# Splitting a norm over two stages, moving two outputs into attention's loop, and unread products in TensorE's waits

## The reference

```
x = x + mha(layernorm(x), ctx, ctx)             # 16 heads, softmax over 64 keys
y = layernorm(x)
h = y + attention(rmsnorm(y, ln1))              # 16 heads of 32, latent q and kv, rope, causal
x = x + h + moe0(rmsnorm(h, ln2))               # 1 shared expert + top 2 of 7, inner width 256
x = x + readout(layernorm(x), ctx, mask)        # softmax(x ctx^T / sqrt(512)) ctx
x = x + moe1(layernorm(x))                      # top 8 of 32 experts, inner width 192
```

## Time and profile before

| what | us |
|---|---|
| median of 3 runs (lowest, highest) | 1833.81 (1829.18, 1837.07) |
| the profiled execution | 1838.66 |
| its span | 1836.8 |
| `cross` and the start, to 93 us: PE clock | 0.73 |
| attention up to 571 us: PE clock | 0.94 |
| 571 to 620 us, end of attention: PE clock | 0.71 |
| 931 to 1088 us, `middle`: PE clock | 0.61 |
| 1139 to 1803 us, moe1: PE clock | 1.00 |

### The profile page before, as it was taken

One profiled execution on the slowest core, in us unless ns is written; L12 is line 12 of the kernel. 1 busy time (PEld: TensorE's weight loads), 2 busy tenths in 40 slices (PEclk: granted clock), 3 DMA queues, 4 the chain that ended last, 5 costly groups with the idle time before them and its releaser, 6 DMA issues. The chain is left out here.

```text
span 1836.8 us, 34150 instructions
## 1 busy us (share of the span) xinstructions
PE 1558.3 (85%) x8796; PEld 1186.7 (65%) x8797; DVE 1360.3 (74%) x2776; ACT 1038.4 (57%) x1969; POOL 786.0 (43%) x542
## 2 busy tenths in 40 slices
PE   4577899898888599999938827999999999999991
PEld 2445667666564477777726526788888787778880
DVE  6735867756675466666637876999999999889992
ACT  1124645534452266666523315888888888788870
POOL 5100010110202323555410124788888888778881
PEclk9588999998989599999976657999999999999996
DMA  9225537344350544765574314888888889888778
GB/s 336 79 53 120 111 69 179 75 116 88 70 138 1 156 163 131 172 136 102 86 219 146 121 60 90 211 187 187 185 192 172 184 186 215 212 208 181 130 124 301
DMA packets 169997, 270.55 MB, mean 147 GB/s; under 512 B 20417, under 2 KB 96193, under 8 KB 168193
## 3 DMA queue, kind: packets, MB, share of 16 engines
q0 software_dynamic: 49008, 117.24, 32.3%
q1 hardware_dynamic: 120896, 152.18, 29.4%
HBM read 153.72 MB, written 89.06 MB: 132 GB/s over the span
## 5 line engine op out<-in xcount | busy, mean ns | idle before, releaser
L1609 DVE TENSOR_TENSOR moe_w_lo<-moe_w_up,moe_w_hi 128x1536 fp32r<-128x1536 f32 (+1 forms) x216 | 408.5, 1891 | 10.0 <-ACT moe_w_hi L1488 10.0
L1429 POOL DMA_INDIRECT moe_rows<-moe_rows,moe_ids x200 | 323.4, 1617 | 67.4 <-issue 57.9
L1488 ACT ACTIVATE moe_w_hi<-moe_w_up 128x1536 fp32r (+3 forms) x216 | 343.3, 1590 | 8.5 <-SPq L1387 8.5
L1704 PE MATMUL psum<-moe_w_hi,moe_rows_hi 128*128 128x384 f32 (+1 forms) x864 | 322.8, 374 | 6.3 <-DVE moe_rows_lo L1603 6.3
L1705 PE MATMUL psum<-moe_w_lo,moe_rows_hi 128*128 128x384 f32 (+1 forms) x864 | 304.5, 352 | 0.0
L1706 PE MATMUL psum<-moe_w_hi,moe_rows_lo 128*128 128x384 f32 (+1 forms) x864 | 304.4, 352 | 0.0
L1730 PE MATMUL psum<-moe_w_down,moe_hid_t 128*128 (+1 forms) x544 | 268.6, 592 | 1.9 <-DVE moe_tail_t L1597 1.3
L1445 POOL DMA_INDIRECT moe_sum<-moe_res,moe_ids x100 | 163.7, 1637 | 100.3 <-ACT moe_res L1531 42.7
L1445 POOL DMA_INDIRECT moe_other<-moe_res,moe_ids x100 | 166.0, 1660 | 87.6 <-ACT moe_res L1531 36.9
L1603 DVE TENSOR_TENSOR moe_rows_lo<-psum,moe_rows_hi 128x512 fp32r<-128x512 f32 x216 | 148.9, 689 | 54.6 <-issue 40.0
L721 ACT ACTIVATE prob<-psum,neg_top 128x128 f32<-128x128 f32 (+3 forms) x256 | 133.3, 528 | 85.0 <-DVE neg_top L851 75.5
(11 more groups left out here) (282 smaller groups left out, 2830.3 us busy)
## 6 DMA issues: line engine op xcount, KB each, us to landing
moe_w_up<-in_L_ffn_w_gate SPq DMA_DIRECT2D x32, 384.0 KB
moe_w_up<-in_L_ffn_w_up SPq DMA_DIRECT2D x32, 384.0 KB
q_st<-q_hi SPq DMA_DIRECT2D x64, 128.0 KB, 2.9
k_st<-k_hi SPq DMA_DIRECT2D x64, 128.0 KB, 3.1
k_st<-k_lo SPq DMA_DIRECT2D x64, 128.0 KB, 3.2
q_st<-q_lo SPq DMA_DIRECT2D x64, 128.0 KB, 3.1
moe_w_down<-in_L_ffn_w_down SPq DMA_DIRECT2D x32, 256.0 KB
moe_w_down<-in_L_ffn_w_down SPq DMA_DIRECT2D x64, 128.0 KB
```

Source lines behind the costliest of these rows:

```text
L1429: pool.indirect_dma_start(rows[u][:, :], None, d["rows"], bass.IndirectOffsetOnAxis(ids[:, t:t + 1], 0)).then_inc(gathered[u], 16)
L1488: sc.activation(w_hi[u % SPLITS][:, :], w_up[:, bass.ds(at * DC, DC), :].rearrange("p a n -> p (a n)"), ACT.Copy).then_inc(T["wh"], 1)
L1609: v.tensor_tensor(w_lo[u % SPLITS][:, :], w_up[:, bass.ds(at * DC, DC), :].rearrange("p a n -> p (a n)"), w_hi[u % SPLITS][:, :].bitcast(F ...
L1704: mm(ps[:, 2 + i, 0:2 * I], hi, w_h, start=(k == 0), stop=False)
```

## The change

Three edits in one. First, `two_norms` takes over POOL's five steps and is called twice: in `cross` for the four tiles of batch 0, as soon as DVE has their variance (in its loop's first round), and in attention's block for the other twelve, behind POOL's first memset; DVE waits for it before the first tile of batch 1. Second, the `normed(1, t)` calls move from before the loop to its first two rounds, two tiles each; and for the last batch the `output` of its first two tiles moves to steps 20 and 24 and their `residual` to steps 22 and 26, with the last tile's output in bank 0 in place of bank 3. Third, `keep_busy` adds products of the identity with 512 columns of constants, written to a PSUM bank that nobody reads then, in full or with half of the columns of the identity (and half of the bank's partitions). It stands at nine places of PE's order: 2 and 2 in attention's end, 3 and 3 at the start of moe0, 2 at that of moe1, and 5, 4, 2 (last batch only) and 2 (each of the other three batches) in `middle`, there with half. No result changes. No line that loads experts is in the diff.

```diff
+def keep_busy(nc, m, c, products, bank, half=False):
+    rows = slice(P // 2, P) if half else slice(0, P)
+    for _ in range(products):
+        nc.tensor.matmul(m["psum"][rows, bank, :], c["ident"][:, rows], m["const"][:, 0:D], start=True, stop=True)
...
+def two_norms(g, own, m, var, mv, rstd, rms, tiles):
+    var, spread, rstd, rms, power = var[:, tiles], mv[:, tiles, 1], rstd[:, tiles], rms[:, tiles], m["power"][:, tiles]
+    own.run(g.tensor_tensor(rstd, var, power, ALU.pow))
+    own.run(g.tensor_tensor(rms, rstd, rstd, ALU.mult))
+    own.run(g.tensor_tensor(rms, rms, spread, ALU.mult))
+    own.run(g.tensor_tensor(rms, rms, m["eps"][:, tiles], ALU.add))
+    return g.tensor_tensor(rms, rms, power, ALU.pow)
...
             pool.wait_ge(S["var"], 1)
-            own.run(g.tensor_tensor(rstd[:, :], var[:, :], m["power"][:, :], ALU.pow))
...
+            own.run(two_norms(g, own, m, var, mv, rstd, rms, slice(0, TPB)))
...
                 stats_of(x(t), t, mv[:, t, :])
+                if b == 0:
+                    own.wait()
+                    v.tensor_scalar(var[:, 0:TPB], mv[:, 0:TPB, 1], EPS, None, ALU.add).then_inc(S["var"], 1)
             own.wait()
-            v.tensor_scalar(var[:, :], mv[:, :, 1], EPS, None, ALU.add).then_inc(S["var"], 1)
+            own.run(v.tensor_scalar(var[:, TPB:TILES], mv[:, TPB:TILES, 1], EPS, None, ALU.add))
...
+        OUT_BANK = lambda b, n: 0 if (b, n) == (LAST, LAST) else 3
...
-            g.memset(r["prob"][:, :, :], -1.0).then_inc(S["zeroed"], 1)
+            g.memset(r["prob"][:, :, :], -1.0).then_inc(S["scales"], 1)
             pool.sem_inc(S["sent"], 1)
+            own = Steps(pool, S["scales"], 1)
+            two_norms(g, own, m, var, mv, rstd, rms, slice(TPB, TILES)).then_inc(S["scales"], 1)
...
                 dve.wait_ge(S["z"], n)
+                if n == TPB:
+                    dve.wait_ge(S["scales"], 6)
...
-                v.tensor_tensor(h[:, t, :], h[:, t, :], ps[:, 3, :], ALU.add).then_inc(S["hres"], 1)
+                v.tensor_tensor(h[:, t, :], h[:, t, :], ps[:, OUT_BANK(b, n), :], ALU.add).then_inc(S["hres"], 1)
...
+                if b == LAST and s in (22, 26):
+                    residual(LAST, s // 4 - 5)
...
-            for t in range(TPB):
-                normed(1, t)
             maxima(*UNITS[0])
             for at in range(len(UNITS) + 4):
                 if at + 1 < len(UNITS):
                     maxima(*UNITS[at + 1])
+                if at < 2:
+                    normed(1, 2 * at)
+                    normed(1, 2 * at + 1)
...
-            for n in range(TPB):
+            for n in range(2, TPB):
                 residual(LAST, n)
...
-                t = QUERY_ORDER[n]
+                t, bank = QUERY_ORDER[n], OUT_BANK(b, n)
...
+                if b == LAST and s in (20, 24):
+                    output(LAST, s // 4 - 5)
...
-            for n in range(TPB):
+            for n in range(2, TPB):
                 output(LAST, n)
+            keep_busy(nc, m, c, 2, 4)
             for t in range(TPB):
                 hidden_flip(LAST, t)
...
             logits(LAST, LAST)
+            keep_busy(nc, m, c, 2, 4)
             ranks(LAST)
...
+            keep_busy(nc, m, c, 3 if SHARED else 2, 6)
             flip(0, 0)
             flip(0, 1)
+            if SHARED:
+                keep_busy(nc, m, c, 3, 6)
             up(0, 0)
...
+            keep_busy(nc, m, c, 5, 5, True)
             xn_flips(0)
             pe.wait_ge(S["cts"], 2)
             scores(0)
+            keep_busy(nc, m, c, 4, 5, True)
             attended(0)
             for b in range(BATCH):
                 if b + 1 < BATCH:
                     xn_flips(b + 1)
                     scores(b + 1)
+                else:
+                    keep_busy(nc, m, c, 2, 5, True)
                 logits(b)
                 if b + 1 < BATCH:
+                    keep_busy(nc, m, c, 2, 5, True)
                     attended(b + 1)
                 run_keys(b)
```

More of the change, by code:

```diff
@@ L300, in write_runs, with cross @@
         pool.indirect_dma_start(table, bass.IndirectOffsetOnAxis(m["run_at"][:, b, t:t + 1], 0), ids, None).then_inc(m["listed1"], 16)
-def cross(nc, a, m, c, dram, s_init, x_first, mv, rstd, rms, weights):
+def two_norms(g, own, m, var, mv, rstd, rms, tiles):
[5 more added lines that the diff above has]
+    return g.tensor_tensor(rms, rms, power, ALU.pow)
+def cross(nc, a, m, c, dram, s_init, x_first, mv, var, rstd, rms, weights):
     ctx = ExitStack()
@@ L326, in cross @@
         stats, mv_q, var_q, rstd_q = sb("stats", [P, TILES, 6]), sb("mv_q", [P, BATCH, 2]), sb("var_q", [P, BATCH]), sb("rstd_q", [P, BATCH])
-        var = sb("var", [P, TILES])
         xn, xn_t = sb("xn", [P, BATCH, D]), sb("xn_t", [P, BATCH, DC, P])
@@ L549, in front @@
         mv, rstd, rms = sb("mv", [P, TILES, 2]), sb("rstd", [P, TILES]), sb("rms", [P, TILES])
-        cross(nc, a, m, c, dram, s_init, x, mv, rstd, rms, [
+        var = sb("var", [P, TILES])
+        cross(nc, a, m, c, dram, s_init, x, mv, var, rstd, rms, [
             (w_kvd[:, :, :], a["L0_ffn_kv_d_w"].rearrange("(c p) n -> p c n", p=P)),
@@ L584, in front @@
         r["slot"], r["entry"] = m["slot0"], m["entry0"]
-        names = ("zeroed z zt zts kvd qd kvds qds pp pr pv_ qkp qkr vs tq tk qts kts qls kls x_in x_back st ntop pexp pt pta ptb pv rden rdt rdts "
+        names = ("scales z zt zts kvd qd kvds qds pp pr pv_ qkp qkr vs tq tk qts kts qls kls x_in x_back st ntop pexp pt pta ptb pv rden rdt rdts "
                  "attd hres acc oproj var2 rms2 hn hnt hnts logit lgs lge masked ranked slotted scattered sent rows_out dve").split()
@@ L1007, in between @@
                     normed(b + 2, s // 2 - 11)
+                if b == LAST and s in (22, 26):
+                    residual(LAST, s // 4 - 5)
                 if done >= 0 and s == 30:
                     route(done, 3)
-            dve.wait_ge(S["zeroed"], 1)
+            dve.wait_ge(S["scales"], 1)
             for t in range(TPB):
@@ L1157, in output @@
             def output(b, n):
-                t = QUERY_ORDER[n]
+                t, bank = QUERY_ORDER[n], OUT_BANK(b, n)
                 pe.wait_ge(S["attd"], b * TPB + n + 1)
-                take(3, "hres", b * TPB + n + 1)
+                take(bank, "hres", b * TPB + n + 1)
                 for k in range(DC):
-                    last = mm(ps[:, 3, :], att_t[:, t, k, :], w_o[:, k, :], start=(k == 0), stop=(k == DC - 1))
+                    last = mm(ps[:, bank, :], att_t[:, t, k, :], w_o[:, k, :], start=(k == 0), stop=(k == DC - 1))
                 last.then_inc(S["oproj"], 1)
```

## The result

The changed kernel takes 1823.56 us (median; 1812.9 to 1842.76), the kernel before, run beside it, 1832.85 (1827.42 to 1837.07). The ratio is 0.9947 [0.9931, 0.9963], 9.7 us faster: just past 0.5%. Three of the new kernel's nineteen times, 1840.68 to 1842.76, lie over 1.5% above its fastest, count as slow and are not in the ratio; the means of all times are only 6.1 us apart. The forecast sum was 14.4, its time 1819.4.

A forecast was written before the change was run, and what follows sets the result against it. PE was taken to bound attention and the expert stages, DVE likelier `middle`; at hand-overs, whoever is waited for last. Terms 5.6 + 2.4 + 1.1 + 1.5 + 0.8 + 3.0 = 14.4 us off 1833.81 gave 1819.4; range 1808 to 1830.

The forecast's parts named there:

- the likeliest case: Whole kernel: the forecast from the summed gains, time 1813 to 1825 us, chance 0.54.
- Term 1: End of `cross`: splitting `two_norms` lets attention start earlier, released by a store instead of POOL; gain 5.6 us.
- Term 2: Attention's start: moving `normed(1, t)` into the loop brings the fifth unit's scores earlier; gain 2.4 us.
- Term 3: Attention's end: two outputs and residuals moved into the last loop cost 7.7, `hidden` comes 8.8 earlier; net gain 1.1 us.
- Term 4: Attention's end: unread products raise the clock, little for the flips and mostly for `ranks`; gain 1.5 us.
- Term 5: Starts of moe0 and moe1: unread products in DMA waits make PE faster in the first tiles; gain 0.8 us.
- Term 6: `middle`: 17 half-width products raise the clock and shorten DVE's waits for PE; gain 3.0 us, between 0 and 8.2.
- Rival A: All unread products: the clock follows them everywhere, gain 23.1 us, time 1811; chance 0.22.
- Rival B: Attention's last loop pays 11 us, its tail saves only 3.4, products change nothing: 1832.5, no measurable change; chance 0.20.
- Rival C: PE's queue: unread products arrive too late or take too long, delaying waited-for work; slower, 1850; chance 0.04.

The follow-up runs named there:

- the reordering alone: Kernel before plus only batch 1's tiles and two last-batch outputs and residuals moved into the loops, last output in bank 0: ratio 1.0018, 3.3 us slower.

## Why the time came out in the range and the gain 4.8 us too high

The measured 1823.56 lies in the range, 1808 to 1830, and just inside the likeliest case, 1813 to 1825. Part of that is luck. In this pair of profiles the stretches whose code is not changed gave +3.58 and -3.64 and happen to cancel; two terms came out too low and three too high. And one pair is little to judge a term of 1 us by, so beside the pair stand the averages over all fourteen profiles.

**Term 1, norms, 5.6: right.** 5.50 in the pair of profiles, by the steps given: POOL is done before DVE, and by the times above the store is late next. In the seven profiles with the split norms attention begins at 86.5 to 88.2, in the seven without at 93.6 to 94.2.

**Term 2, the tiles in the loop, 2.4: right in kind, low.** 3.56. In the eight profiles with this edit the stage is 58.8 to 60.3 us, in the six without 62.3 to 64.5, so about 4. Whether all of it lasts to the end is open (below).

**Term 3, attention's end, 1.1: the sign is wrong in the pair, and the better choice was missed.** Cost 9.26 for 7.7, gain 7.63 for 8.8, net -1.6. The prediction's sign for it, a time from the loop's start to the last `hidden` unchanged beyond term 2, did not show: from the fifth unit's scores to `hidden` it grew by 5.2 us, 3.58 of them in batches whose code is not changed. Over all profiles the last loop takes 98.3 us on average with four outputs behind it in one bank (six kernels, 95.3 to 101.6) and 104.4 with two in it (six, 101.2 to 107.8): 6.1. The tail is 25.2 and 17.5: 7.6. Both terms of the sum were sized within 1.6 us, and their difference, 1.5, is near the 1.1. In two banks and behind the loop they are 99.7 and 18.9. So most of the tail's gain, 6.3 of 7.6, comes from the second bank, which costs little (1.4 us between the loop's averages, less than their spread), and the move buys the other 1.4 for some 5. Loop and tail together, in the four kernels of the second chip: 122.0 and 122.9 with the move, 118.2 and 118.9 without it.

**Term 4, attention's end, 1.5: 0.46.** The row that I took to speak for `ranks` did not decide: PE was busy from 596 to 605 at 0.54, then with the two products, and the clock stayed at 0.50. In the three of seven kernels with these products where it rose, this stage is 9.15 instead of 10.78: the 1.6 is right when it comes. Logits and `ranks` together take 21.9 us in each of the seven kernels without products here and 18.6 to 21.5, on average 20.5, in the seven with them: 1.4, near the forecast, though the lowest two have the other tail as well.

**Term 5, expert stages, 0.8: 1.76** (1.45 and 0.31). The flips ran at full clock, 0.66 us for the earlier trace rows's 1.11, and so did the unread products behind them; in the first tile's products the clock fell again. PE's timeline in the changed kernel:

```profile
621.46 0.66 PE L1712 MATMUL psum<-const_sb,moe_rows 128*128 128x128 f32 x4 [0.45 <-DMA moe_rows<-moe_rows]
...
623.65 2.74 PE L212 MATMUL psum<-const_sb 128*128 128x512 f32 x6
...
633.65 0.63 PE L1733 MATMUL psum<-moe_w_hi,moe_rows_lo 128*128 128x512 f32 x1
```

Over all profiles the two places are 0.7 us shorter with the products, with ranges that overlap (moe0's first gate 17.7 to 19.8 with, 18.3 to 20.0 without), so the 1.76 of the pair is in part chance and the 0.8 was well sized.

**Term 6, `middle`, 3.0: this step failed; it gave -0.1.** With terms 2 to 5 off by +1.2, -2.7, -1.0 and +1.0, it makes up 3.1 of the 4.8. The reasoning was that DVE waits 8.2 us for PE, that the clock either follows or does not, and that the products themselves cost at most half a microsecond each time, hidden by DVE. The clock followed in part: 34 us at full clock became 55. From the residual of batch 0 to that of batch 1, and from there to that of batch 2, the stage gained 2.2 and 3.1 us by it (22.72 for 24.96, 26.32 for 29.40). But then this follows in the changed kernel:

```profile
999.00:1009.70 10.70, 8.18 (x58) 6.17 (x57) 9.50 (x41) 3.48 (x8) 1.05 (x1) 1.00 0.32 117
1009.70:1054.10 44.40, 43.67 (x131) 28.32 (x132) 33.25 (x136) 11.62 (x19) 8.88 (x9) 0.50 0.43 134
```

At 1009.7 the clock falls, and for 44.4 us it stays at 1.2 GHz (0.50) with PE busy 43.67 of them. The third batch's scores fall into it, DVE is not the bound there any more (busy 23.61 of 33.32), and 6.8 us are lost: 33.32 for 26.53 up to the residual of batch 3. The last stretch gives 1.4 back.

These 6.8 us have two parts, and the changed kernel without `middle`'s products separates them. There too one batch falls wholly into half clock; first its window, then PE and DVE in the same place of the changed kernel:

```profile
1013.46:1043.90 30.44, 29.76 (x113) 23.53 (x112) 23.70 (x99) 9.19 (x16) 5.19 (x6) 0.50 0.53 167
```

```profile
1036.71 0.42 DVE L2003 TENSOR_TENSOR m_att<-m_att,m_den 128x256 f32<-128x256 f32 x1
...
1038.28 3.68 PE L212 MATMUL psum<-const_sb 128*64 128x512 f32 x4
...
1041.89 1.06 PE L2145 MATMUL psum<-const_sb,m_att 128*64 128x128 f32 x4
```

DVE has the shares ready at 1037.13, but PE, late by its half clock, comes to them only behind the pair of unread products: 3.68 us with no wait to cover them. So about 3.9 of the 6.8 us are the half clock (30.44 for 26.53) and 2.9 are the products' own time (33.32 for 30.44). It holds in every profile in which a batch falls wholly, or all but wholly, into half clock: 30.4 to 30.6 us in six kernels without the products, 33.1 to 33.5 in the five with them.

That such a batch is PE's could be seen beforehand. Two windows of the kernel before, up to the residuals of batches 3 and 2:

```profile
1023.90:1050.40 26.50, 21.53 (x113) 15.61 (x112) 23.55 (x99) 8.69 (x15) 4.87 (x5) 0.69 0.61 189
994.50:1023.90 29.40, 25.87 (x114) 19.70 (x112) 23.77 (x100) 11.72 (x20) 3.13 (x4) 0.62 0.53 168
```

An estimate from them: wholly at half clock PE's work would take 21.53 x 0.69 / 0.50 = 30 and 25.87 x 0.62 / 0.50 = 32 us, and DVE's takes 24. I had priced full clock at every wait and never half clock at a place that had been full, where a product also has no wait to hide in. The Trainium skill ("TensorE: Matmul & The Clock Gate", section "What's actually happening") has a sustained busy stretch take the array to 2.4 GHz; by that rule these 44 us would be at full clock. The window from 1009.70 to 1054.10 disagrees, more sharply than rows 8 did: 98% busy, half clock. Why the clock fell at 1009.7 is not settled, nor what brought it back at 1054.1.

**Rival A** (the clock follows everywhere, 1811) is out by the same windows. **Rival B** was nearer to the loop's price in this pair, 9.26 between 7.7 and 11, but not on average (6.1), and not to the tail's. **Rival C** did not come about as a slower kernel, but its mechanism occurred at one place: the pair of products in the half-clock batch of `middle`, 2.9 us of their own time.

## What the loops of attention showed

The +3.58 us between the fifth unit's scores and batch 3, where the code is not changed (+0.82 in batch 0, +2.89 in batch 1, -0.13 in batch 2), and the wide spread of the new kernel's times led me to compare the same stretch in all profiles. From the first scores of batch 1 to those of batch 2 the fourteen executions took 110.8 to 117.2 us, and the granted clock tells them apart: 110.9 at 1.00, 112.2 at 0.98, 114.1 at 0.97, 117.0 at 0.94. The single times of the changed kernel go along with the clock of the whole execution too: 0.916 to 0.921 in the eleven up to 1825.67 us, 0.909 to 0.916 in the eight from 1826.72. The windows of batches 1 and 2 and of the stretch where they part, in the changed kernel:

```profile
286.00:300.00 14.00, 13.30 (x57) 9.66 (x57) 4.97 (x10) 4.32 (x13) 0.00 (x0) 0.51 0.75 177
230.01:347.04 117.03, 108.21 (x852) 78.50 (x850) 82.60 (x199) 57.68 (x174) 6.09 (x5) 0.94 0.45 112
347.04:469.19 122.15, 111.31 (x850) 79.51 (x850) 78.74 (x196) 56.36 (x171) 14.09 (x13) 0.92 0.40 96
```

and in the kernel with the unread products alone, the same stretches:

```profile
297.00:311.00 14.00, 12.25 (x112) 9.19 (x116) 10.77 (x22) 6.93 (x20) 0.00 (x0) 1.00 0.69 179
241.01:351.92 110.91, 102.01 (x851) 74.19 (x850) 82.67 (x199) 57.69 (x174) 6.09 (x5) 1.00 0.46 118
351.92:462.20 110.28, 101.71 (x850) 74.26 (x850) 78.58 (x196) 56.25 (x171) 14.17 (x13) 1.00 0.45 106
```

Both stretches begin with one wait of PE for `q_lo`. PE's timeline, in the changed kernel and then in the other:

```profile
286.69 1.09 PE L1082 MATMUL psum<-const_sb,h 128*128 128x128 f32 x4 [1.26 <-DVE q_lo L917]
```

```profile
297.77 0.63 PE L1072 MATMUL psum<-const_sb,h 128*128 128x128 f32 x4 [1.33 <-DVE q_lo L910]
```

The same instructions after a wait of the same length, once at 1.2 GHz for 13 us, once at 2.4. PE is the bound in this loop, so such a fall costs about 6 us, and up to 12 us a batch (batch 2: 110.3 to 122.3). One such fall is as much as the largest term of the prediction. The clock of 0.94 in batch 1 was seen in four of the eight kernels with the tiles moved (term 2) and in none of the six others (lowest 0.97). That may mean that term 2 gives back at batch 1 and 2 what it gains at the start, and would agree with the 1.0018 of the moved tiles alone, whose profile has 117.05 and 122.08 us there. With one profile a kernel it is not shown, and stays open. So does the cause of the DVE stalls at the `att_t` copy behind the loop (3.80 us in the changed kernel, 5.31 with two banks, 1.34 with the reordering alone and in the changed kernel without unread products). Nor is the clock all of it: the rest of moe1 and `finish`, behind every edit, took from 692.8 us in the changed kernel to 702.7 with the norms alone, and I have no cause for that.

## The version to keep

All four outputs behind the loop in two banks, with the norms split, the tiles moved and the products kept: 0.9919 [0.9886, 0.9951] of the kernel before. It beats that one clearly. Against the changed kernel (0.9947 [0.9931, 0.9963]) the intervals overlap. The four kernels of the second chip can be compared directly: two with two outputs in the loop have a mean of 1828.1 us over 24 times, two with all four behind it in two banks 1821.4 over 17, a difference of 6.7 with a 95% interval of about 3 to 10. So the better order of the tail is shown; the windows above give the reason for some 4 us of it. Whether `middle`'s products should stay is not: the pair is 2.8 us apart within its intervals. A kernel without the pairs ahead of `attended`, whose own time showed in the half-clock batch, is not among the runs.

## What to carry to other kernels

Where consumers wait for one another through one buffer, a second buffer costs less than moving half of the work into a loop that is 93% busy. A norm whose scales the next stage needs in parts should be computed in the order of need: 5.5 us here. Price a change of clock in both directions, at each place where the slower engine would become the bound, and price unread products there with nothing to hide them. Divide the span at the same instructions before believing a difference, and take more than one profile for a term of 1 us: stretches whose code had not changed differed by up to 12 us.

## What was not expected of the hardware

A stretch of 44.4 us at half clock with PE busy 43.67 us of it, 98%. The same wait of 1.3 us in the same instructions, followed by half clock in one execution and by full clock in another. And unread products of half width, with which PE was about as long at full clock as with full ones: 55 and 58 us.
